# Adding Q rows to gathered P rows inside the gathering DMA, in a graph-attention kernel

## The chip, the cores and the metric

The kernel runs on one core of a Trainium2 chip. The time is the device time of one execution, in microseconds (us). Engines are named as the profile names them: PE (TensorE), DVE (VectorE), ACT (ScalarE), POOL (GpSimd), SP (SyncE); beside them 16 DMA engines move data.

## The reference

There are 512 nodes with 1024 features, and 8704 edges sorted by destination. With h = relu(layernorm(x)), each edge has a logit from its two end nodes, by a weight matrix that depends on the edge's position: the first 256 edges are "hh", the next 1280 "oo", the remaining 7168 "ho".

```python
feat = concat([h[src], h[dst]], axis=1)
e_f  = relu(feat[part] @ W_part + b_part)        # W_part: 2048 x 1024, for hh, oo, ho
logit = (e_f @ W_a + b_a)[:, 0]
alpha = softmax of logit over the edges with the same dst
z = segment_sum(alpha[:, None] * h[src], dst)
out = x + concat([relu([h, z][:128] @ W_hn + b_hn), relu([h, z][128:] @ W_on + b_on)])
```

## The kernel before

**The split of the edge product.** For ho and oo the product of an edge is a sum of two node products: P = h @ W[top half] + b, looked up by src, and Q = h @ W[bottom half], looked up by dst. Both tables, 512 rows of 1024 float32 (4 KB), are made once per kind (`p_ho`, `q_ho`, `p_oo`, `q_oo` in device memory). An edge's logit is then the sum over the features of relu(P[src] + Q[dst]) * w_a. The 256 hh edges are multiplied directly.

**Edge tiles.** A tile is 128 edges, one on each partition. ho has 56 tiles (`T_HO`), oo 10 (`T_OO`), together `T_NODE` = 66; each partition holds a run of consecutive edges (partition p, columns 0 to 55), so that in a run the destination often repeats. `column(n)` (L51) gives the column of tile n: with four slots, each slot walks along a run of its own. For each tile POOL issues three indirect DMAs on its one queue: `p_rows` (L843 to L847) gathers 128 P rows into `gath[:, 0, slot]`; `q_rows` (L849 to L854) gathers Q rows into `gath[:, 1, slot]`; `scatter` (L856 to L859) writes the 128 logits into a 512 x 512 table of pairs. `q_rows` takes its indices from `q_index` (L445 to L450), in which an edge whose destination is that of the slot's last edge has an index out of bounds: that row isn't moved, and the Q row that lies in the slot is used again.

**DVE's part** is `edges(n)` (L464 to L473): it waits for both rows, adds them (L470), and L472 does relu, the product with w_a and the sum in one instruction.

**POOL's order** is written out (L861 to L897): P of tiles 0 to 3 once the P table is stored, Q of tiles 0 to 3 once Q is stored (L866), then for each n from 4: wait for the logits of tile n-4, issue P(n), Q(n), wait until all earlier scatters have landed (`s_scat`), scatter(n-4). In between stand the two hh scatters (`HH_AT`) and the loads of the pair tables.

**DVE's order** is written out too. In the counting stage (L521 to L524) 16 tiles stand between the one-hots (L502) that PE needs to count pairs (L714). Then the weight chunks come: a chunk (1 MB, `raw`, loaded by SP at L204) is split by ACT into a high part (`split_hi`, L240) and by DVE into a low part (`split_lo`, L424), and PE multiplies with both (L664 to L666, three matmuls for each product). `TILES_OO`, `TILES_HH`, `TILES_TOP` and `TILES_G` say how many tiles DVE does before each chunk's `split_lo`: three for each of the 8 chunks of the oo stage, 10 in the hh stage (8 chunks, half the matmuls), 10 in the 8 chunks of the node update's top half, and 2 before each of the first three chunks of the stage after it. So a late gather delays DVE's next `split_lo`, and that delays PE.

**The end.** When all logits are scattered, the tables are loaded, maxima, exponentials and counts give the attention matrix, and PE multiplies it (L810 to L812).

Of the kernel before, what the change touches and what calls it, by code (L numbers as in the profile page):

```python
# [16 lines left out]
P = 128  # L17
N, D = 512, 1024
# [6 lines left out]
T_HH, T_OO, T_HO = E_HH // P, E_OO // P, E_HO // P  # L25
T_ALL = T_HO + T_OO + T_HH
T_NODE = T_HO + T_OO
# [12 lines left out]
ORDER = (1, 2, 3, 0)  # L40
SLOTS = 4
RUN = T_HO // SLOTS
OO_RUNS = (0, 3, 6, 8)
HH_AT = 58
UNCHANGED = 1024.0
EMPTY = -3.0e38
TINY = 1.0e-30
EPS = 1e-5


def column(n):  # L51

    if n < T_HO:
        return RUN * (n % SLOTS) + n // SLOTS
    n -= T_HO
    return T_HO + OO_RUNS[n % SLOTS] + n // SLOTS


def build(nc, x, src, dst, w_chunks, biases, w_a, b_a, out):
    f32, f32r, bf16, f16 = mybir.dt.float32, mybir.dt.float32r, mybir.dt.bfloat16, mybir.dt.float16  # L60
    i32, i16 = mybir.dt.int32, mybir.dt.int16
    ALU = mybir.AluOpType
# [11 lines left out]
    with ExitStack() as ctx:  # L74
        def sb(name, shape, dt):
            return ctx.enter_context(nc.sbuf_tensor(name, shape, dt))
# [9 lines left out]
        def sem(name):  # L86
            return ctx.enter_context(nc.semaphore(name))
# [5 lines left out]
        w_lo = sb("w_lo", [P, SPLIT, KC, HALF], f32r)  # L93
        gath = sb("gath", [P, 2, SLOTS, D], f32)
        feat_hi, partial = shared(("feat_hi", [P, 2 * KT, E_HH], f32r), ("partial", [P, NB, D], f32))
# [25 lines left out]

        q_index = sb("q_index", [P, T_NODE], i32)
        cell = sb("cell", [P, T_NODE], i32)
        logit = sb("logit", [P, T_NODE], f32)
        same = sb("same", [P, T_NODE], f32)
        pair_hh = sb("pair_hh", [P, T_HH], i32)
# [7 lines left out]

        edge_p, edge_q = gath[:, 0], gath[:, 1]
        x_sb = gath[:, 0]
# [19 lines left out]
        s_qrow = [sem(f"q_rows_landed{i}") for i in range(SLOTS)]  # L156
        s_esum, s_logit, s_scat = sem("edge_summed"), sem("logit_ready"), sem("logits_scattered")
        s_node = sem("node_row_ready")
# [229 lines left out]
        def _(dve):  # L388
            steps = [0]

            def step(i):

                steps[0] += 1
                i.then_inc(s_dve, 1)
                dve.wait_ge(s_dve, steps[0])
# [48 lines left out]

            step(nc.vector.tensor_tensor(same[:, 1:T_NODE], f_dst[:, 1:T_NODE], f_dst[:, 0:T_NODE - 1], ALU.is_equal))  # L445
            for first in (*range(0, T_HO, RUN), *(T_HO + at for at in OO_RUNS)):
                i = nc.vector.memset(same[:, first:first + 1], 0.0)
            step(i)
            nc.vector.scalar_tensor_tensor(out=q_index[:, :], in0=same[:, :], scalar=UNCHANGED, in1=f_dst[:, 0:T_NODE],
                                           op0=ALU.mult, op1=ALU.add)  # L450
            nc.vector.scalar_tensor_tensor(out=cell[:, :], in0=f_dst[:, 0:T_NODE], scalar=float(N),
# [12 lines left out]
            def edges(n):  # L464

                slot, at = n % SLOTS, column(n)
                dve.wait_ge(s_prow[slot], 16 * (n // SLOTS) + 16)
                dve.wait_ge(s_qrow[slot], 16 * (n // SLOTS) + 16)
                p, q = edge_p[:, slot], edge_q[:, slot]
                nc.vector.tensor_tensor(p, p, q, ALU.add).then_inc(s_esum, 1)  # L470
                dve.wait_ge(s_esum, n + 1)
                nc.vector.scalar_tensor_tensor(out=p, in0=p, scalar=0.0, in1=wa[:, :], op0=ALU.max, op1=ALU.mult,  # L472
                                               accum_out=logit[:, at:at + 1]).then_inc(s_logit, 1)  # L473

# [341 lines left out]
        def _(pool):  # L816
# [26 lines left out]
            def p_rows(n):  # L843
                kind, slot, at = "ho" if n < T_HO else "oo", n % SLOTS, column(n)
                nc.gpsimd.indirect_dma_start(edge_p[:, slot], None, node_tab[kind][0][:, :],  # L845
                                             bass.IndirectOffsetOnAxis(ap=i_src[:, at:at + 1], axis=0)
                                             ).then_inc(s_prow[slot], 16)  # L847

            def q_rows(n):  # L849

                kind, slot, at = "ho" if n < T_HO else "oo", n % SLOTS, column(n)
                nc.gpsimd.indirect_dma_start(edge_q[:, slot], None, node_tab[kind][1][:, :],  # L852
                                             bass.IndirectOffsetOnAxis(ap=q_index[:, at:at + 1], axis=0),
                                             bounds_check=N - 1, oob_is_err=False).then_inc(s_qrow[slot], 16)  # L854

            def scatter(n):  # L856
                kind, at = "ho" if n < T_HO else "oo", column(n)
                nc.gpsimd.indirect_dma_start(pair_tab[kind][:, :], bass.IndirectOffsetOnAxis(ap=cell[:, at:at + 1], axis=0),  # L858
                                             logit[:, at:at + 1], None).then_inc(s_scat, 16)  # L859

# [5 lines left out]
            pool.wait_ge(s_qst, 32)  # L866
            for n in range(SLOTS):
                q_rows(n)
            for n in range(SLOTS, T_NODE + SLOTS):
# [13 lines left out]
                if n < T_NODE:  # L883
                    p_rows(n)
                    q_rows(n)
                if n > SLOTS:
# [44 lines left out]
```

## Time and profile before

| | us |
|---|---|
| median of 3 runs (567.0 to 568.1) | 567.56 |
| the profiled execution | 567.12 |
| its span, first to last instruction | 565.3 |
| PE busy | 481.7 |
| DVE busy | 360.5 |
| POOL busy | 271.3 |
| ACT busy | 173.3 |
| data moved | 111.27 MB |

The profiled execution agrees with the runs. A matmul's end is modelled in this profile, so PE's busy time is not time at its peak rate. A POOL `DMA_INDIRECT` is the time in which POOL makes the descriptors; the transfer itself runs afterwards in the DMA engines, and "to landing" is the time from issue until its semaphore rises.

### The profile page before, as it was taken

The numbers are of one execution on the slowest core, as the hardware profiler recorded it, in microseconds if no ns is written. First come the engines' busy times: TensorE is split into PE (matmuls) and PEld (weight loads), VectorE is DVE, ScalarE is ACT, GpSimd is POOL, SyncE is SP. The second block draws the span as 40 slices with busy tenths as digits, with TensorE's granted clock in tenths as the row PEclk, the third lists the DMA queues.
The fourth block names the chain that finished last, engine by engine and source line by source line (L and its number), as shares of the span: only waits on it lengthen the run. The fifth ranks groups of instructions, "written<-read, shape, count | busy, mean of one in ns | idle before, by whom it ended". The sixth has DMA issues, their size and how long they took to land.

```text
span 565.3 us, 5665 instructions
## 1 busy us (share of the span) xinstructions
PE 481.7 (85%) x2008; PEld 361.7 (64%) x2008; DVE 360.5 (64%) x516; ACT 173.3 (31%) x236; POOL 271.3 (48%) x221
## 2 busy tenths in 40 slices
PE   2799999989989899897785579786867999999397
PEld 2688888833434488676664467574745888888285
DVE  5713133249987687656675688797874567657644
ACT  3611321457764611221014023222212121443400
POOL 2020000326887867667766777776766563303000
PEclk9999999989998899989988689898989999999689
DMA  8998254762444455766587578678767943200412
GB/s 332 384 425 312 88 177 166 275 222 79 119 117 120 122 182 170 258 235 193 186 266 251 185 241 259 223 251 267 253 233 278 362 154 113 74 1 0 150 56 93
DMA packets 38196, 111.27 MB, mean 197 GB/s; under 512 B 13542, under 2 KB 13542, under 8 KB 32672
## 3 DMA queue, kind: packets, MB, share of 16 engines
q0 software_dynamic: 22576, 45.93, 26.1%
q1 hardware_dynamic: 9888, 53.03, 25.2%
q10 hardware_dynamic: 5712, 12.06, 5.9%
q8 instruction: 11, 0.18, 0.1%
q14 instruction: 9, 0.07, 0.0%
HBM read 123.80 MB, written 15.76 MB: 247 GB/s over the span
## 4 chain that ended last, share of the span: by engine, by line
PE 38%; POOL 25%; issue 15%; DMA 11%; DVE 9%; ACT 1%; POOLq 0%; ACTq 0%; DVEq 0%
PE bank L664 11%; PE bank L666 11%; PE bank L665 11%; POOL pairs_ho L858 9%; POOL gath L845 8%; POOL gath L852 8%; DMA gath<-q_ho,q_index 6%; DMA pairs_ho<-logit,cell 2%; DVE gath L470 2%; DVE gath L472 2%; DVE w_lo L424 2%; PE bank L714 2%; DMA gath<-q_oo,q_index 1%; PE bank L810 1%; PE bank L811 1%
## 5 line engine op out<-in xcount | busy, mean ns | idle before, releaser
L664 PE MATMUL bank<-w_hi,h_t 128*128 128x512 f32 x448 | 180.2, 402 | 30.9 <-DVE w_lo L424 28.6
L665 PE MATMUL bank<-w_lo,h_t 128*128 128x512 f32 x448 | 179.2, 400 | 0.0
L666 PE MATMUL bank<-w_hi,h_t 128*128 128x512 f32 x448 | 178.5, 398 | 0.0
L240 ACT ACTIVATE w_hi<-raw 128x1024 fp32r<-128x1024 f32 x80 | 80.5, 1054 | 276.2 <-PE bank L666 245.8
L424 DVE TENSOR_TENSOR w_lo<-raw,w_hi 128x1024 fp32r<-128x1024 f32 x80 | 95.1, 1228 | 67.5 <-ACT w_hi L240 67.5
L470 DVE TENSOR_TENSOR gath<-gath 128x1024 f32<-128x1024 f32 x66 | 80.9, 1226 | 83.4 <-DMA gath<-q_ho,q_index 58.7
L664 PEld LDWEIGHTS bank<-w_hi,h_t 128*128 128x128 f32 x448 | 86.8, 194 | 54.1 <-DVE w_lo L424 29.2
L845 POOL DMA_INDIRECT gath<-p_ho,i_src x56 | 68.3, 1220 | 89.8 <-DMA p_ho<-stage 65.5
L858 POOL DMA_INDIRECT pairs_ho<-logit,cell x56 | 76.8, 1371 | 48.3 <-DMA pairs_ho<-logit,cell 37.3
L666 PEld LDWEIGHTS bank<-w_hi,h_t 128*128 128x128 f32 x448 | 86.9, 194 | 18.5
L665 PEld LDWEIGHTS bank<-w_lo,h_t 128*128 128x128 f32 x448 | 86.5, 193 | 18.0
L472 DVE SCALAR_TENSOR_TENSOR gath<-gath,wa 128x1024 f32<-128x1024 f32 x66 | 81.1, 1230 | 2.3
L852 POOL DMA_INDIRECT gath<-q_ho,q_index x56 | 69.2, 1236 | 27.9 <-issue 16.8
L714 PE MATMUL bank<-count_buf 128*128 128x512 bf16 x272 | 66.0, 401 | 3.1 <-DVE count_buf L502 2.6
L714 PEld LDWEIGHTS bank<-count_buf 128*128 128x128 bf16 x272 | 26.5, 102 | 41.7 <-DVE count_buf L502 8.9
L292 ACT ACTIVATE count_buf<-node_row,step_at 128x512 bf16<-128x512 f16 x68 | 45.2, 714 | 25.0 <-PE bank L714 25.0
L664 PE MATMUL bank<-w_hi,feat_hi 128*128 128x512 f32 x64 | 28.8, 450 | 20.3 <-DVE w_lo L424 20.3
L664 PEld LDWEIGHTS bank<-w_hi,feat_hi 128*128 128x128 f32 x64 | 13.7, 214 | 25.1 <-DVE w_lo L424 17.8
L665 PE MATMUL bank<-w_lo,feat_hi 128*128 128x512 f32 x64 | 28.1, 438 | 0.0
L666 PE MATMUL bank<-w_hi,feat_lo 128*128 128x512 f32 x64 | 27.5, 430 | 0.0
L502 DVE TENSOR_SCALAR count_buf<-node_row,f_dst 128x512 bf16<-128x512 f16 x68 | 21.6, 364 | 8.4 <-PE bank L714 8.0
L858 POOL DMA_INDIRECT pairs_oo<-logit,cell x10 | 13.5, 1350 | 20.3 <-DMA pairs_oo<-logit,cell 19.4
(118 smaller groups left out, 314.0 us busy)
## 6 DMA issues: line engine op xcount, KB each, us to landing
raw<-w_chunks SPq DMA_DIRECT2D x40, 1024.0 KB, 6.9
gath<-x SPq DMA_DIRECT2D x4, 512.0 KB, 5.1
h_dram<-h_sb SPq DMA_DIRECT2D x1, 2048.0 KB, 14.0
p_ho<-stage ACTq DMA_DIRECT2D x2, 1024.0 KB, 5.5
q_ho<-stage ACTq DMA_DIRECT2D x2, 1024.0 KB, 4.2
p_oo<-stage ACTq DMA_DIRECT2D x2, 1024.0 KB, 8.7
q_oo<-stage ACTq DMA_DIRECT2D x2, 1024.0 KB, 5.4
x_again<-x ACTq DMA_DIRECT2D x2, 1024.0 KB, 6.6
```

Source lines behind the costliest of these rows:

```text
L240: nc.scalar.activation(w_hi[:, c % SPLIT, k], raw[:, c % RAW, k], ACT.Copy).then_inc(s_whi, 1)
L292: i = nc.scalar.activation(rows[:, slot, j, 0], node_row[:, :], ACT.Sign, bias=step_at[:, bass.ds(2 * g + j, 1)])
L424: nc.vector.tensor_tensor(w_lo[:, c % SPLIT, k], raw[:, c % RAW, k], w_hi[:, c % SPLIT, k].bitcast(f32), ALU.subtract).then_inc(s_wlo, 1)
L470: nc.vector.tensor_tensor(p, p, q, ALU.add).then_inc(s_esum, 1)
L472: nc.vector.scalar_tensor_tensor(out=p, in0=p, scalar=0.0, in1=wa[:, :], op0=ALU.max, op1=ALU.mult, accum_out=logit[:, at:at + 1]).then_in ...
L664: nc.tensor.matmul(to, hi, w_hi[:, slot, k], start=first, stop=False)
L665: nc.tensor.matmul(to, hi, w_lo[:, slot, k], start=False, stop=False)
L666: return nc.tensor.matmul(to, lo, w_hi[:, slot, k], start=False, stop=last)
L714: i = nc.tensor.matmul(bank[banks + b][:, :], rows[:, slot, j, 1, b * P:(b + 1) * P], rows[:, slot, j, 0], start=False, stop=False)
L845: nc.gpsimd.indirect_dma_start(edge_p[:, slot], None, node_tab[kind][0][:, :], bass.IndirectOffsetOnAxis(ap=i_src[:, at:at + 1], axis=0)). ...
L852: nc.gpsimd.indirect_dma_start(edge_q[:, slot], None, node_tab[kind][1][:, :], bass.IndirectOffsetOnAxis(ap=q_index[:, at:at + 1], axis=0) ...
L858: nc.gpsimd.indirect_dma_start(pair_tab[kind][:, :], bass.IndirectOffsetOnAxis(ap=cell[:, at:at + 1], axis=0), logit[:, at:at + 1], None). ...
```

## The change

The Q rows have no buffer of their own. `gath` is used as eight slots of one tile each. POOL gathers P(n) into a slot, later waits until it has landed, and issues an indirect DMA with `compute_op=ALU.add`, which adds the Q rows, by dst, to what lies in the slot. DVE's add and the indices that skip repeated Q rows are gone: every Q row of every tile is fetched. The add of tile n-2 (`BEHIND`) is issued after P(n); P runs eight tiles ahead of DVE instead of four. The columns are taken in plain order.

```diff
--- before.py
+++ after.py
@@ -38,22 +38,12 @@
 TILES_G = [2, 2, 2, 0, 0, 0, 0]
 PEAK_HH, PEAK_HO = 3, 4
 ORDER = (1, 2, 3, 0)
-SLOTS = 4
-RUN = T_HO // SLOTS
-OO_RUNS = (0, 3, 6, 8)
+SLOTS = 8
+BEHIND = 2
 HH_AT = 58
-UNCHANGED = 1024.0
 EMPTY = -3.0e38
 TINY = 1.0e-30
 EPS = 1e-5
-
-
-def column(n):
-
-    if n < T_HO:
-        return RUN * (n % SLOTS) + n // SLOTS
-    n -= T_HO
-    return T_HO + OO_RUNS[n % SLOTS] + n // SLOTS
 
 
 def build(nc, x, src, dst, w_chunks, biases, w_a, b_a, out):
@@ -91,7 +81,7 @@
 
         x_again, w_hi = shared(("x_again", [P, NHALF, NB, HALF], f32), ("w_hi", [P, SPLIT, KC, HALF], f32r))
         w_lo = sb("w_lo", [P, SPLIT, KC, HALF], f32r)
-        gath = sb("gath", [P, 2, SLOTS, D], f32)
+        gath = sb("gath", [P, 2, SLOTS // 2, D], f32)
         feat_hi, partial = shared(("feat_hi", [P, 2 * KT, E_HH], f32r), ("partial", [P, NB, D], f32))
         feat_lo, g_on_left, hh_rows, h_sb = shared(("feat_lo", [P, 2 * KT, E_HH], f32r),
                                                    ("g_on_left", [P, 2, NB, HALF], f32r),
@@ -119,10 +109,8 @@
         step_at = sb("step_at", [P, T_ALL], f32)
         f_dst = sb("f_dst", [P, T_ALL], f32)
 
-        q_index = sb("q_index", [P, T_NODE], i32)
         cell = sb("cell", [P, T_NODE], i32)
         logit = sb("logit", [P, T_NODE], f32)
-        same = sb("same", [P, T_NODE], f32)
         pair_hh = sb("pair_hh", [P, T_HH], i32)
         logit_half = sb("logit_half", [P, NHALF, T_HH], f32)
         logit_hh = sb("logit_hh", [P, T_HH], f32)
@@ -132,7 +120,7 @@
         peak = sb("peak", [P, 8, NB], f32)
         den = sb("den", [P, 2, NB], f32)
 
-        edge_p, edge_q = gath[:, 0], gath[:, 1]
+        edge = gath[:, :, :, :].rearrange("p a s d -> p (a s) d")
         x_sb = gath[:, 0]
 
         tab_sb = [stage[:, 0], gath[:, 0, 0:2, :].rearrange("p a (b n) -> p (a b) n", n=N), stage[:, 1]]
@@ -154,7 +142,7 @@
         s_one, s_oused, s_cnt, s_cev = sem("onehot_ready"), sem("onehot_used"), sem("counted"), sem("counts_evacuated")
         s_prow = [sem(f"p_rows_landed{i}") for i in range(SLOTS)]
         s_qrow = [sem(f"q_rows_landed{i}") for i in range(SLOTS)]
-        s_esum, s_logit, s_scat = sem("edge_summed"), sem("logit_ready"), sem("logits_scattered")
+        s_logit, s_scat = sem("logit_ready"), sem("logits_scattered")
         s_node = sem("node_row_ready")
         s_hhlog, s_hhscat = sem("hh_logits_ready"), sem("hh_scattered")
         s_hhev, s_hhhalf = sem("hh_evacuated"), sem("hh_half_logits")
@@ -442,12 +430,6 @@
             step(nc.vector.tensor_copy(f_dst[:, :], i_dst[:, :]))
             nc.vector.tensor_scalar(step_at[:, :], f_src[:, :], -1.0, 0.5, ALU.mult, ALU.add)
 
-            step(nc.vector.tensor_tensor(same[:, 1:T_NODE], f_dst[:, 1:T_NODE], f_dst[:, 0:T_NODE - 1], ALU.is_equal))
-            for first in (*range(0, T_HO, RUN), *(T_HO + at for at in OO_RUNS)):
-                i = nc.vector.memset(same[:, first:first + 1], 0.0)
-            step(i)
-            nc.vector.scalar_tensor_tensor(out=q_index[:, :], in0=same[:, :], scalar=UNCHANGED, in1=f_dst[:, 0:T_NODE],
-                                           op0=ALU.mult, op1=ALU.add)
             nc.vector.scalar_tensor_tensor(out=cell[:, :], in0=f_dst[:, 0:T_NODE], scalar=float(N),
                                            in1=f_src[:, 0:T_NODE], op0=ALU.mult, op1=ALU.add)
             nc.vector.scalar_tensor_tensor(out=pair_hh[:, :], in0=f_dst[:, T_NODE:T_ALL], scalar=float(N),
@@ -463,14 +445,11 @@
 
             def edges(n):
 
-                slot, at = n % SLOTS, column(n)
-                dve.wait_ge(s_prow[slot], 16 * (n // SLOTS) + 16)
+                slot = n % SLOTS
                 dve.wait_ge(s_qrow[slot], 16 * (n // SLOTS) + 16)
-                p, q = edge_p[:, slot], edge_q[:, slot]
-                nc.vector.tensor_tensor(p, p, q, ALU.add).then_inc(s_esum, 1)
-                dve.wait_ge(s_esum, n + 1)
-                nc.vector.scalar_tensor_tensor(out=p, in0=p, scalar=0.0, in1=wa[:, :], op0=ALU.max, op1=ALU.mult,
-                                               accum_out=logit[:, at:at + 1]).then_inc(s_logit, 1)
+                nc.vector.scalar_tensor_tensor(out=edge[:, slot], in0=edge[:, slot], scalar=0.0, in1=wa[:, :],
+                                               op0=ALU.max, op1=ALU.mult, accum_out=logit[:, n:n + 1]
+                                               ).then_inc(s_logit, 1)
 
             split_lo(2)
             split_lo(3)
@@ -841,22 +820,23 @@
                                ).then_inc(s_tab[kind], 16)
 
             def p_rows(n):
-                kind, slot, at = "ho" if n < T_HO else "oo", n % SLOTS, column(n)
-                nc.gpsimd.indirect_dma_start(edge_p[:, slot], None, node_tab[kind][0][:, :],
-                                             bass.IndirectOffsetOnAxis(ap=i_src[:, at:at + 1], axis=0)
+                kind, slot = "ho" if n < T_HO else "oo", n % SLOTS
+                nc.gpsimd.indirect_dma_start(edge[:, slot], None, node_tab[kind][0][:, :],
+                                             bass.IndirectOffsetOnAxis(ap=i_src[:, n:n + 1], axis=0)
                                              ).then_inc(s_prow[slot], 16)
 
-            def q_rows(n):
-
-                kind, slot, at = "ho" if n < T_HO else "oo", n % SLOTS, column(n)
-                nc.gpsimd.indirect_dma_start(edge_q[:, slot], None, node_tab[kind][1][:, :],
-                                             bass.IndirectOffsetOnAxis(ap=q_index[:, at:at + 1], axis=0),
-                                             bounds_check=N - 1, oob_is_err=False).then_inc(s_qrow[slot], 16)
+            def add_q_rows(n):
+
+                kind, slot = "ho" if n < T_HO else "oo", n % SLOTS
+                pool.wait_ge(s_prow[slot], 16 * (n // SLOTS) + 16)
+                nc.gpsimd.indirect_dma_start(edge[:, slot], None, node_tab[kind][1][:, :],
+                                             bass.IndirectOffsetOnAxis(ap=i_dst[:, n:n + 1], axis=0),
+                                             compute_op=ALU.add).then_inc(s_qrow[slot], 16)
 
             def scatter(n):
-                kind, at = "ho" if n < T_HO else "oo", column(n)
-                nc.gpsimd.indirect_dma_start(pair_tab[kind][:, :], bass.IndirectOffsetOnAxis(ap=cell[:, at:at + 1], axis=0),
-                                             logit[:, at:at + 1], None).then_inc(s_scat, 16)
+                kind = "ho" if n < T_HO else "oo"
+                nc.gpsimd.indirect_dma_start(pair_tab[kind][:, :], bass.IndirectOffsetOnAxis(ap=cell[:, n:n + 1], axis=0),
+                                             logit[:, n:n + 1], None).then_inc(s_scat, 16)
 
             pool.wait_ge(s_tabs, 48)
             pool.wait_ge(s_norm, 2)
@@ -864,8 +844,8 @@
             for n in range(SLOTS):
                 p_rows(n)
             pool.wait_ge(s_qst, 32)
-            for n in range(SLOTS):
-                q_rows(n)
+            for n in range(SLOTS - BEHIND):
+                add_q_rows(n)
             for n in range(SLOTS, T_NODE + SLOTS):
                 if n == T_HO:
                     pool.wait_ge(s_pst, 64)
@@ -882,7 +862,8 @@
                 pool.wait_ge(s_logit, n - SLOTS + 1)
                 if n < T_NODE:
                     p_rows(n)
-                    q_rows(n)
+                if n - BEHIND < T_NODE:
+                    add_q_rows(n - BEHIND)
                 if n > SLOTS:
                     pool.wait_ge(s_scat, 16 * (n - SLOTS))
                 scatter(n - SLOTS)
```

## Rows read from the trace of the kernel before

**Rows 1.** The page: busy time of each engine; the costliest groups, busy and mean | idle before.

```profile
PE 481.7 (85%) x2008; PEld 361.7 (64%) x2008; DVE 360.5 (64%) x516; ACT 173.3 (31%) x236; POOL 271.3 (48%) x221
...
L470 DVE TENSOR_TENSOR gath<-gath 128x1024 f32<-128x1024 f32 x66 | 80.9, 1226 | 83.4 <-DMA gath<-q_ho,q_index 58.7
```

**Rows 2.** Waits, 199 to 434 us: who waited for whom, total us, times, longest.

```profile
DVE gath L470 <- DMA gath<-q_ho,q_index: 53.8, 20, 5.6
...
PE bank L664 <- DVE w_lo L424: 45.2, 13, 8.4
POOL pairs_ho L858 <- DMA pairs_ho<-logit,cell: 37.3, 20, 3.1
...
DVE gath L470 <- DMA gath<-q_oo,q_index: 10.9, 2, 7.4
```

**Rows 3.** Timeline of PE: start us, us, engine, line, operation.

```profile
197.20 0.39 PE L666 MATMUL bank<-w_hi,h_t 128*128 128x512 f32 x1
...
204.68 0.39 PE L666 MATMUL bank<-w_hi,h_t 128*128 128x512 f32 x1
```

**Rows 4.** Groups of PE's instructions by line, 199 to 434 us; L665, L666 have like counts.

```profile
L664 PE MATMUL bank<-w_hi,h_t 128*128 128x512 f32 x185 | 75.7, 409 | 24.9 <-DVE w_lo L424 24.8
...
L664 PE MATMUL bank<-w_hi,feat_hi 128*128 128x512 f32 x64 | 28.8, 450 | 20.3 <-DVE w_lo L424 20.3
```

**Rows 5.** Stretches: length, busy of each engine; last columns clock, DMA share, GB/s.

```profile
0.00:50.00 50.00, 36.57 (x150) 30.60 (x151) 24.59 (x61) 18.73 (x26) 7.13 (x14) 1.00 0.91 369
199.00:316.00 117.00, 94.00 (x387) 75.35 (x385) 80.57 (x96) 22.18 (x26) 81.65 (x68) 0.94 0.65 214
...
434.00:480.00 46.00, 44.43 (x189) 36.70 (x190) 32.24 (x40) 7.97 (x10) 26.43 (x21) 0.96 0.59 210
```

**Rows 6.** POOL's three issues: duration min/median/max ns; last row P's landings.

```profile
L845 POOL DMA_INDIRECT gath<-p_ho,i_src x56: 937/966/2016, 101.2 to 397.3; - x56
...
L852 POOL DMA_INDIRECT gath<-q_ho,q_index x56: 986/1005/2062, 117.7 to 398.5; - x56
...
L858 POOL DMA_INDIRECT pairs_ho<-logit,cell x56: 1025/1034/2080, 133.5 to 432.1; - x56
...
DMA to landing us min/median/max: 4.1/5.2/10.3
```

**Rows 7.** Timelines of POOL and DVE near 350 us.

```profile
351.39 1.00 POOL L852 DMA_INDIRECT gath<-q_ho,q_index  x1 [0.31 <-issue]
...
357.41 2.00 POOL L852 DMA_INDIRECT gath<-q_ho,q_index  x1 [0.31 <-issue]
...
356.12 2.41 DVE L424 TENSOR_TENSOR w_lo<-raw,w_hi 128x1024 fp32r<-128x1024 f32 x2
```

**Rows 8.** DMA, 199 to 434 us: totals; queues' packets, MB, share; P gathers issued.

```profile
DMA packets 19192, 54.78 MB, mean 233 GB/s; under 512 B 7766, under 2 KB 7766, under 8 KB 16240
...
q0 software_dynamic: 13472, 25.32, 35.1%
q1 hardware_dynamic: 3312, 24.12, 28.8%
q10 hardware_dynamic: 2400, 5.24, 6.3%
...
gath<-p_ho,i_src POOLq DMA_INDIRECT x37, 5.4
gath<-p_oo,i_src POOLq DMA_INDIRECT x4, 5.1
```

**Rows 9.** Groups of DVE's instructions by line: one that prepares the Q indices.

```profile
L445 DVE TENSOR_TENSOR same<-f_dst 128x65 f32<-128x65 f32 x1 | 0.2, 221 | 0.0
```

**Rows 10.** Counting stage: DVE's groups, 127 to 191 us; PE's count matmuls, all.

```profile
L470 DVE TENSOR_TENSOR gath<-gath 128x1024 f32<-128x1024 f32 x16 | 19.5, 1219 | 4.9 <-DMA gath<-q_ho,q_index 4.9
L502 DVE TENSOR_SCALAR count_buf<-node_row,f_dst 128x512 bf16<-128x512 f16 x58 | 18.4, 362 | 4.1 <-PE bank L714 3.6
...
L714 PE MATMUL bank<-count_buf x272: 376/379/635, 118.3 to 192.3; 128*128 128x512 bf16 x136
```

## The prediction

> **What bounds the kernel now.** I first read the shares of busy time. PE is busy 85% of the span, DVE 64%, POOL 48% [rows 1]. No engine is full over the whole span, so the limit has to be found stage by stage. The DVE add that the change deletes (L470) is 66 instructions of 1226 ns, 80.9 us of DVE time, and DVE stood idle 83.4 us just before them, mostly for Q rows to land [rows 1].
>
> Second, the waits inside the long stretch from 199 to 434 us, where chunks 9 to 33 of the weights meet tiles 16 to 58 of the edges [rows 2]. PE waits 45.2 us for DVE's `split_lo` (L424). DVE waits 53.8 + 10.9 = 64.7 us for gathers. POOL waits 37.3 us for its previous scatter to land. So the chain is POOL and its transfers, then DVE, which runs its tiles and its splits in one written order, then PE.
>
> Third, how much PE has to give. In an unbroken piece the matmul at 197.20 and the one at 204.68 are 33 matmuls apart, 0.227 us each [rows 3]. The stretch records 185 x 3 + 64 x 3 = 747 of them [rows 4], so PE needs 747 x 0.227 = 169 us of the 235. Up to 66 us could be won there, if DVE never came late. From 434 to 480 PE is busy 44.4 of 46 us [rows 5], so the tail is PE's own and I leave it as it is.
>
> Fourth, what POOL does. An issue costs 0.966 us for P (L845), 1.005 for Q (L852), 1.034 for the scatter (L858) [rows 6], with 0.30 us of sequencer time before each. That is 3.9 us a tile at best, against 235 / 43 = 5.5 us taken. Part of the rest is contention: at 351.39, with DVE waiting, L852 takes 1.00 us; at 357.41, under the `TENSOR_TENSOR` of L424, it takes 2.00 [rows 7].
>
> Fifth, the DMA engines. In the stretch they moved 54.78 MB and the three queues show 35.1 + 28.8 + 6.3 = 70% of the 16 engines' time [rows 8], 233 GB/s. They are not the bound yet, but landings are long (P 5.2 us in the median, up to 10.3) [rows 6].
>
> **The change part by part.**
>
> Removed on DVE: L470 and its wait, 1.23 us a tile, 43 tiles in the stretch: 53 us of work. DVE is waiting for rows more than that (64.7 us), so this alone wins nothing while rows come no sooner.
>
> Removed with it: the preparation of `q_index` and `same`, one 0.22 us operation [rows 9] and ten of its size or smaller, under 1 us in all, beside PE's first products. Nothing.
>
> POOL's contention: with L470 gone only L424 can stretch an issue. In 199 to 316 POOL's 68 issues took 81.65 us [rows 5], 1.20 each against 1.0 in the medians, so 0.6 us a tile is lost, and more in the later part. L470 and L424 run about equally often there, so I count half of the loss as gone; what L424 still costs I put at 0.4 us a tile. POOL's floor is then 3.9 + 0.4 = 4.3 us a tile.
>
> Slots: eight tiles deep instead of four. P of tiles 4 to 7 is issued in the gap between 106 and 117.7 us, where POOL waited for the Q store, instead of after it, so 4 x 1.27 = 5 us come off POOL's chain at the start, and later bursts of landing time are ridden out.
>
> Added wait: POOL now waits for P(n-2) to land before it issues the add for n-2. Behind it stand that add, the scatter of n-8 and P(n+1); DVE and the scatter's own successor wait for those. P(n-2) is two rounds, 2 x 5.5 = 11 us, older; the median landing is 5.2, the maximum 10.3. Covered: zero. If P landings double, each excess microsecond is POOL's.
>
> Added bytes, the largest term. Today a Q row is skipped when the edge before it in the partition had the same destination. In the stretch queue 0 moved 25.32 MB; 41 P gathers of 128 x 4 KB are 21.5 and one table is 1.05, so Q moved only 2.8 MB for 42 gathers [rows 8]. Afterwards each is whole, 22.0 MB: 19.2 MB more. And each row is not copied but added: the engine must fetch the Q row and also fetch the P row that stands in the slot. No row shows such a transfer. The low bound is a plain gather, 74.0 MB in all for the stretch; two fetches make it 96.0; a high bound is a gather's time three times, 118 MB. I take two fetches, since two rows have to be read for one written.
>
> Rate of the engines: in the first 50 us 369 GB/s at a share of 0.91 [rows 5], which is 405 at 1.0; in the stretch 233 at 0.70, which is 331 at 1.0 (its packets include waiting in contention). I take the middle, 370. Then 96.0 MB need 259 us, where the stretch takes 235: **+24 us**. The ends: 237 us (+2) at 405, 290 us (+55) at 331. The work of one tile there is 259 / 43 = 6.0 us, above POOL's 4.3 and PE's 169 / 43 = 3.9, so the engines set the pace.
>
> On this point the trace is silent and the Trainium skill is not: "Collectives: The Full Stack" (The bandwidth ceiling, on why ReduceScatter is half of AllGather) says that an add in the DMA engine costs no ALU time but needs two source reads in the same read ring, and so runs at half the rate of a copy. By that page the sum is the +24 above, by a free add it would be the first rival.
>
> The counting stage, 120 to 191 us: DVE alternates one-hots (58 x 0.36 us) and 16 tiles, of which the add is 1.2 us each [rows 10], and PE's 272 count matmuls need only 272 x 0.227 = 62 us of its 74. There are no weight loads; P and the add are 3 x 0.524 = 1.57 MB a tile, 4.2 us at 370, and POOL's 3.9 is near it. Six adds can be issued from 117.7; the last 10 tiles at 4.2 us end at about 125 + 42 + 6 = 173, so PE becomes the bound and the stage ends near 184: **-7 us**. Bounds -10 and 0.
>
> Sum: 24 - 7 = +17. The profiled execution took 567.1 us (span 565.3 and 1.8 around it), 0.4 below the median of 567.56. 567.1 + 17 = **584**.
>
> **Rivals.**
>
> Forecast's case, two fetches, the engines the bound, 0.55. Its own range is 235 to 290 us for the stretch less 7 (or 0): 562 to 622.
>
> An add as cheap as a plain gather, 0.30. For it: the engines' share is only 0.70 today, and nothing in the trace excludes that the second fetch, which is from on-chip memory, runs beside the first. Then 74.0 MB at 370 are 200 us, POOL's 43 x 4.3 + 5 for the two scatters of HH are 190, PE's 169 is below: the stretch falls by 35, and with the 7 the time is 525 (549 at 331 GB/s, 515 if POOL alone counts). The case decides below about 1.6 fetches per add: (235 x 0.370 - 52) / 22 = 1.6, where 52 MB is everything but the adds.
>
> An add dearer than two fetches, 0.15. Its place is either the engines (three fetches: 118 / 0.370 = 319 us, +84, near 650) or POOL's issue, if it has to write more than one descriptor per row on the reading side: an add of 3.0 us instead of 1.0 makes 43 x 6.3 = 271 us, +36, near 600. I price it at 630. Against it: nothing in the trace; for it: only that there is no row.
>
> The order of the adds against P (two tiles behind) as a bound of its own would need P to land later than 11 us; that is a consequence of saturated engines and is inside the first and third case.
>
> **How the numbers follow.** A measurement of this kernel can tell 0.2%, 1.1 us, from no change. The forecast case gives slower 0.47, no difference 0.03, faster 0.05 (its low end plus the counting stage); the cheap add is faster, 0.30; the dear one slower, 0.15. Together 0.35, 0.03, 0.62. Both signs have weight. The range takes most of the cheap case and part of the dear one, 518 to 636; the likeliest case's own is 562 to 622.
>
> **What the changed profile would show.** DMA share near 0.95 in 199 to 434, queue 0 with about 75 MB by the bytes it writes and a time share above 45%; DVE at L472 still waiting over 60 us, for adds; L852's successor at about 1.0 us an issue, landing in 7 us or more; scatters landing in 5 us or more; tile 15 done near 173 to 180 us. If instead DMA share stays near 0.8, PE's waits for L424 shrink from 45 us below 20 and tile 58 is done before 400 us, the cheap case holds and 584 is wrong by the doubled fetch. If POOL's adds last 2 us or more each, the dear one holds.

## The result and the profile after

The changed kernel takes 626.88 us (621.55 to 632.55, 4 runs) against 567.83 (567.0 to 568.69): the ratio is 1.103, interval 1.093 to 1.114, 59 us slower. The forecast was 584, slower; the sign came true, and the loss was three and a half times the forecast one. One of the four runs, 632.55, was in a slower state of the chip; without it the median is 624.86 and the loss 57 us.

The page of the changed kernel, to be read against [rows 1]: its span, busy shares, the slices of DMA share, the queues, and the chain that ended last.

```profile
span 627.1 us, 5463 instructions
...
PE 494.9 (79%) x2008; PEld 370.2 (59%) x2008; DVE 280.7 (45%) x440; ACT 173.3 (28%) x236; POOL 296.5 (47%) x221
...
DMA  9995328899988899988899899899969997401302
...
q0 software_dynamic: 22576, 74.50, 49.6%
...
DMA 45%; PE 28%; POOL 15%; issue 7%; DVE 4%; ACT 1%; ACTq 0%; DVEq 0%; POOLq 0%
DMA pairs_ho<-logit,cell 42%; PE bank L643 7%; PE bank L645 7%; PE bank L644 7%; POOL gath L832 5%; POOL pairs_ho L838 4%; POOL gath L824 4%; PE bank L693 2%; DMA gath<-q_oo,i_dst 2%; PE bank L789 1%; PE bank L790 1%; PE bank L791 1%; DMA pairs_hh<-logit_hh,pair_hh 1%; DVE stats L388 1%; POOL pairs_oo L838 1%
```

DVE's 80 us are gone and DMA share is at 0.8 to 0.9 from the first gather on. The surprise is the last line: 42% of the span's chain is one kind of transfer, the scatter of 128 four-byte logits. It moves next to nothing.

Groups of POOL's and DVE's instructions (columns as in [rows 1]), and who waited for whom over the whole span, as in [rows 2].

```profile
L450 DVE SCALAR_TENSOR_TENSOR gath<-gath,wa 128x1024 f32<-128x1024 f32 x66 | 80.8, 1224 | 223.3 <-DMA gath<-q_ho,i_dst 174.1
L832 POOL DMA_INDIRECT gath<-q_ho,i_dst x56 | 90.5, 1615 | 26.2 <-issue 16.8
...
DVE gath L450 <- DMA gath<-q_ho,i_dst: 174.1, 46, 8.8
PE bank L643 <- DVE w_lo L412: 95.4, 18, 11.4
POOL pairs_ho L838 <- DMA pairs_ho<-logit,cell: 91.2, 40, 5.8
```

DVE, relieved of an add, now waits 223 us before its tiles where it waited 83 [rows 1]. POOL waits 91 us for ho scatters and, on a line not shown, 23 for oo ones: 114 against 57 (37 and 19) before.

The stretch from 199 to 434 us, with the columns of [rows 5], and the tiles that DVE finished in it (this answer's groups by line):

```profile
199.00:434.00 235.00, 160.79 (x606) 127.10 (x605) 93.72 (x129) 40.21 (x44) 150.10 (x107) 0.83 0.94 254
...
L450 DVE SCALAR_TENSOR_TENSOR gath<-gath,wa 128x1024 f32<-128x1024 f32 x36 | 44.1, 1225 | 141.2 <-DMA gath<-q_ho,i_dst 141.2
```

36 tiles in 235 us are 6.5 us each, where 43 were done before, 5.5 each. When DVE's tiles start, first and last, tells that the whole loss lies there: before (L472) and in the changed kernel (L450).

```profile
L472 DVE SCALAR_TENSOR_TENSOR gath<-gath,wa x66: 1224/1225/1274, 128.9 to 477.8; 128x1024 f32<-128x1024 f32 x66
L450 DVE SCALAR_TENSOR_TENSOR gath<-gath,wa x66: 1206/1226/1268, 126.8 to 541.0; 128x1024 f32<-128x1024 f32 x66
```

The last tile starts 63 us later, and what comes behind it takes 86 us in place of 88. The granted TensorE clock is hardly the cause: its mean in the stretch fell from 0.93 to 0.83 of full speed, but PE stood idle 74 of the 235 us there (47 before), for `split_lo`, and DVE waits for ACT's high parts 67.5 us in all, as before. The stretch in the kernel before:

```profile
199.00:434.00 235.00, 187.51 (x747) 148.96 (x745) 168.48 (x198) 52.28 (x56) 164.06 (x128) 0.93 0.70 233
```

The chain of waits between 230 and 262 us shows the mechanism, start and length of each piece:

```profile
230.93 6.55 DMA pairs_ho<-logit,cell
237.48 0.27 issue
237.75 8.35 DMA pairs_ho<-logit,cell
246.10 0.27 issue
246.37 6.39 DMA pairs_ho<-logit,cell
```

Each piece runs from a scatter's issue to its landing, and the next scatter starts at once. POOL's own timeline of the same moment:

```profile
237.75 1.00 POOL L838 DMA_INDIRECT pairs_ho<-logit,cell  x1 [2.23 <-DMA pairs_ho<-logit,cell]
239.06 0.96 POOL L824 DMA_INDIRECT gath<-p_ho,i_src  x1 [0.30 <-issue]
240.33 1.56 POOL L832 DMA_INDIRECT gath<-q_ho,i_dst  x1 [0.30 <-issue]
246.37 1.64 POOL L838 DMA_INDIRECT pairs_ho<-logit,cell  x1 [4.48 <-DMA pairs_ho<-logit,cell]
```

The scatter issued at 237.75 stands on the same queue as the rows and adds issued before it. POOL issues one P, one add, and has then to wait 4.48 us until it has landed. (These are among the longer ones; the median of all 66 is below.) One round trip of a scatter per tile is a floor for the tile rate, whatever DVE does.

### The profile page after: what moved, and what is told of

Read it like the earlier page. It is cut to its first block, busy times and chain, and to the rows that moved or that the text cites. A ratio compares the mean times of both kernels' runs of the same rounds, so it can differ in the third digit from the quotient of the medians.

```text
span 627.1 us, 5463 instructions
## 1 busy us (share of the span) xinstructions
PE 494.9 (79%) x2008; PEld 370.2 (59%) x2008; DVE 280.7 (45%) x440; ACT 173.3 (28%) x236; POOL 296.5 (47%) x221
## 3 DMA queue, kind: packets, MB, share of 16 engines
q0 software_dynamic: 22576, 74.50, 49.6%
## 4 chain that ended last, share of the span: by engine, by line
DMA 45%; PE 28%; POOL 15%; issue 7%; DVE 4%; ACT 1%; ACTq 0%; DVEq 0%; POOLq 0%
DMA pairs_ho<-logit,cell 42%; PE bank L643 7%; PE bank L645 7%; PE bank L644 7%; POOL gath L832 5%; POOL pairs_ho L838 4%; POOL gath L824 4%; PE bank L693 2%; DMA gath<-q_oo,i_dst 2%; PE bank L789 1%; PE bank L790 1%; PE bank L791 1%; DMA pairs_hh<-logit_hh,pair_hh 1%; DVE stats L388 1%; POOL pairs_oo L838 1%
## 5 line engine op out<-in xcount | busy, mean ns | idle before, releaser
L643 PE MATMUL bank<-w_hi,h_t 128*128 128x512 f32 x448 | 186.5, 416 | 61.8 <-DVE w_lo L412 59.6
L644 PE MATMUL bank<-w_lo,h_t 128*128 128x512 f32 x448 | 183.5, 410 | 0.0
L645 PE MATMUL bank<-w_hi,h_t 128*128 128x512 f32 x448 | 182.8, 408 | 0.0
L450 DVE SCALAR_TENSOR_TENSOR gath<-gath,wa 128x1024 f32<-128x1024 f32 x66 | 80.8, 1224 | 223.3 <-DMA gath<-q_ho,i_dst 174.1
L643 PEld LDWEIGHTS bank<-w_hi,h_t 128*128 128x128 f32 x448 | 89.9, 201 | 87.1 <-DVE w_lo L412 60.1
L838 POOL DMA_INDIRECT pairs_ho<-logit,cell x56 | 81.7, 1458 | 96.1 <-DMA pairs_ho<-logit,cell 91.2
L412 DVE TENSOR_TENSOR w_lo<-raw,w_hi 128x1024 fp32r<-128x1024 f32 x80 | 94.3, 1220 | 67.5 <-ACT w_hi L228 67.5
L832 POOL DMA_INDIRECT gath<-q_ho,i_dst x56 | 90.5, 1615 | 26.2 <-issue 16.8
L645 PEld LDWEIGHTS bank<-w_hi,h_t 128*128 128x128 f32 x448 | 89.7, 200 | 20.1
L644 PEld LDWEIGHTS bank<-w_lo,h_t 128*128 128x128 f32 x448 | 90.1, 201 | 19.1
L824 POOL DMA_INDIRECT gath<-p_ho,i_src x56 | 62.6, 1118 | 80.4 <-DMA p_ho<-stage 63.6
L693 PE MATMUL bank<-count_buf 128*128 128x512 bf16 x272 | 64.4, 397 | 4.9 <-DVE count_buf L481 4.9
L838 POOL DMA_INDIRECT pairs_oo<-logit,cell x10 | 12.2, 1223 | 26.8 <-DMA pairs_oo<-logit,cell 23.3
L832 POOL DMA_INDIRECT gath<-q_oo,i_dst x10 | 18.3, 1834 | 3.0 <-issue 3.0
```

Source lines behind the costliest of these rows:

```text
L412: nc.vector.tensor_tensor(w_lo[:, c % SPLIT, k], raw[:, c % RAW, k], w_hi[:, c % SPLIT, k].bitcast(f32), ALU.subtract).then_inc(s_wlo, 1)
L450: nc.vector.scalar_tensor_tensor(out=edge[:, slot], in0=edge[:, slot], scalar=0.0, in1=wa[:, :], op0=ALU.max, op1=ALU.mult, accum_out=logi ...
L643: nc.tensor.matmul(to, hi, w_hi[:, slot, k], start=first, stop=False)
L644: nc.tensor.matmul(to, hi, w_lo[:, slot, k], start=False, stop=False)
L645: return nc.tensor.matmul(to, lo, w_hi[:, slot, k], start=False, stop=last)
L693: i = nc.tensor.matmul(bank[banks + b][:, :], rows[:, slot, j, 1, b * P:(b + 1) * P], rows[:, slot, j, 0], start=False, stop=False)
```

## The experiments

Two theories stood at the start: A, the engines' time for the second fetch; B, the round trip of the scatter. A third, C, was POOL's dearer issue (1.57 us in the median for the add, 1.005 for Q before [rows 6]).

**Plain Q gathers in the changed kernel** (the sum is left out):

```diff
                 nc.gpsimd.indirect_dma_start(edge[:, slot], None, node_tab[kind][1][:, :],
                                              bass.IndirectOffsetOnAxis(ap=i_dst[:, n:n + 1], axis=0),
-                                             compute_op=ALU.add).then_inc(s_qrow[slot], 16)
+                                             ).then_inc(s_qrow[slot], 16)
```

> The kernel after, with the add taken out of the Q transfer: it gathers every Q row plainly over the P row in the same slot, with the same waits (the sum P + Q is left out). Theory A (the engines' time for the second fetch is the bound): queue 0's work per tile falls from two kinds of packets, 159 and 328 ns, to two of 159 ns, 3.9 to 2.5 us of all 16 engines, and most of the 59 us comes back: 560 to 580 us. Theory B (POOL waits for each scatter to land, whatever is in the queue, and the round trip of that wait is the bound): the landing of a scatter shortens only by what stands ahead of it, some 1.4 us a tile of 6 to 7, and the time stays near 600 us. Theory C (POOL's dearer issue, 1.57 against 1.0 us, is the bound): the issue falls back to 1.0 and the time falls by 66 x 0.57 = 38 us or less, to about 590.

Measured 569.32 us, ratio 1.003 (0.999 to 1.007): with the same bytes written, the same rows fetched and the same waits, 58 us come back, which is all that the change had lost and no more. Queue 0 of its page:

```profile
q0 software_dynamic: 22576, 74.50, 37.7%
```

The same line of the kernel before:

```profile
q0 software_dynamic: 22576, 45.93, 26.1%
```

From the shares, an added row can be priced. Before, queue 0 moved 45.93 MB in 26.1% of 16 x 565.3 us; here 74.50 MB in 37.7% of 16 x 570.9. The difference is 1083 engine-us for 28.57 MB, 6975 rows of 4 KB: 155 ns a plain row. In the changed kernel the same queue has 49.6% of 16 x 627.1, 1533 engine-us more for the 66 x 128 adds: 181 ns each on top. An add is 155 + 181 = 336 ns, 2.2 plain rows; these are estimates, since a packet's time includes waiting. The packet records say the same: with plain gathers most rows of queue 0 take 159 ns each, and with the add a second group of them takes 328, 2.1 times. So the forecast's doubled fetch was right, and yet the cheap add gave 569 and not the forecast 525. Something other than the engines held it there.

**All Q rows in the kernel before:**

```diff
-            nc.vector.scalar_tensor_tensor(out=q_index[:, :], in0=same[:, :], scalar=UNCHANGED, in1=f_dst[:, 0:T_NODE],
+            nc.vector.scalar_tensor_tensor(out=q_index[:, :], in0=same[:, :], scalar=0.0, in1=f_dst[:, 0:T_NODE],
```

> The kernel before, with every Q row fetched (no index out of bounds), four slots, DVE's add kept. It shows what the 28 MB of Q rows cost by themselves. Theory A: the engines have room at 70% share for plain rows, so 567 to 580 us. Theory B: each scatter lands later by a Q gather's 1.3 us and POOL waits for it, up to 66 x 1.3 = 85 us less what is hidden: 590 to 620.

592.22 us, ratio 1.047 (1.035 to 1.058). The 28.6 MB by themselves cost 24 us, although the DMA share in 199 to 434 was only 0.82. B's range began at 590 and A's ended at 580. What B says of the scatters can be read in four kernels that all have one chain of them. The landing is the time from a scatter's issue to the last rise of its semaphore, the median over the tiles:

| kernel | landing, us | POOL's waits for scatters, us | time, us |
|---|---|---|---|
| before | 3.2 | 57 | 568 |
| before, all Q rows | 4.3 | 77 | 592 |
| changed, plain Q gathers | 4.1 | 74 | 569 |
| changed | 5.6 | 114 | 627 |

The more work the queue has, the later the same 512 bytes land. The time follows with one exception: the changed kernel with plain gathers has no add on DVE and twice the slots.

**Two chains of scatters in the changed kernel** (odd tiles' logits go to a table that is not loaded):

```diff
-                nc.gpsimd.indirect_dma_start(pair_tab[kind][:, :], ...
-                                             logit[:, n:n + 1], None).then_inc(s_scat, 16)
+                nc.gpsimd.indirect_dma_start((pair_tab, odd_tab)[n % 2][kind][:, :], ...
+                                             logit[:, n:n + 1], None).then_inc(s_scat[n % 2], 16)
...
-                if n > SLOTS:
-                    pool.wait_ge(s_scat, 16 * (n - SLOTS))
+                if n > SLOTS + 1:
+                    pool.wait_ge(s_scat[(n - SLOTS) % 2], 16 * ((n - SLOTS) // 2))
```

> The kernel after, with odd tiles' logits scattered into a second pair table with a semaphore of its own, so that a scatter waits for the one two tiles earlier and no longer for the last one (half of the logits are left out of the result). Theory A: the engines are full, so POOL's wait moves elsewhere and the time stays within 10 us of 627. Theory B: POOL's 114 us of waits for scatters go and the time falls to 580 to 600.

577.12 us, ratio 1.016 (1.006 to 1.027): 50 us less than the changed kernel, in a kernel that does the same transfers. A is refuted as the only bound, and B's range, 580 to 600, was a little too high. POOL's waits for scatters fall from 114 to 27 us, while a scatter's median landing rises from 5.6 to 8.2: it is the broken wait that helps, not a faster scatter into a second table. What is left is A's, as the stretch, the slices and queue 0 of its page say:

```profile
199.00:434.00 235.00, 179.52 (x677) 141.04 (x676) 109.69 (x148) 47.25 (x52) 175.19 (x122) 0.86 1.01 293
...
DMA  8997334979999999999999999999979994200412
...
q0 software_dynamic: 22576, 74.50, 50.8%
```

Now the engines are full: a share of 1.01 (packets' times can overlap, so it can pass 1), 40 tiles in 235 us, 5.9 each. The forecast had reckoned 6.0 for exactly this state. The step from 0.94 and 6.5 us a tile looks small; a share close to 1 doesn't by itself say that the engines set the pace.

**The same in the kernel before:**

> The same second table and semaphore in the kernel before (half of the logits are left out of the result). There POOL waits 57 us for scatters. Theory B, for this kernel: it falls by 10 to 30 us, since DVE waits 83 us for Q rows that POOL issues late. Theory A has no say here; if it stays at 567, the waits for scatters were covered even before.

538.51 us, ratio 0.954 (0.945 to 0.964): 29 us faster by the medians, 26 by the ratio. In the stretch DVE finishes 48 tiles instead of 43 (in the profiled execution, 530.57 us, the fastest of the four), and PE waits for `split_lo` 19.9 us in all:

```profile
DVE gath L471 <- DMA gath<-q_ho,q_index: 36.1, 20, 4.2
...
PE bank L665 <- DVE w_lo L425: 19.9, 10, 5.4
```

So the wait for scatters, 37 us in [rows 2], was a bound before the change already, and I had read that row and not priced it.

**Plain gathers and two chains together:**

> Plain Q gathers in the kernel after (the sum left out) and odd tiles' logits in a second table with a semaphore of its own. By the forecast's arithmetic for a cheap add, 74 MB at 370 GB/s, this should be 525. B2 says the same from the runs: with neither the double fetch (3.9 to 2.5 us a tile) nor the scatter's round trip, POOL's issue of 3.9 to 4.3 us is the bound as in the run of the kernel before with two chains (538.5), so 525 to 545. If double fetch and round trip were two bounds in series, their gains add: 627 - 58 - 50 = 519.

535.39 us, ratio 0.939 (0.930 to 0.948). Only with both does the rival's 525 come near. The gains, 58 and 50, don't add: their sum would give 519. With two chains the add costs 577 - 535 = 42, with one chain 58. PE is now busy 215 of the 235 us and 48 tiles take 4.9 us each, so POOL's issue of 3.9 to 4.3 us is not the bound that I expected; PE's own work is near.

```profile
199.00:434.00 235.00, 214.65 (x900) 173.03 (x900) 135.23 (x182) 62.33 (x70) 171.40 (x140) 0.96 0.93 348
```

**Four slots in the changed kernel** (`SLOTS = 4`):

> The kernel after with four slots instead of eight (BEHIND stays 2, so an add can be only two tiles ahead of DVE). Theory B2 (after the first four runs: the engines and the scatter's round trip set POOL's pace, some 6.7 us a tile, and DVE waits for rows all the time): depth is worth little in the steady state, 627 to 645. Rival: depth rides out the long landings, and without it the add's 8 us round trip is seen at every second tile: 660 to 720.

636.71 us, ratio 1.125 (1.116 to 1.134). Half the depth costs 10 us. In the long stretch DVE does 36 tiles with either depth; the last count matmul starts at 203.6 us, against 193.3 with eight slots. Eight slots help little where the supply is late on every tile.

**DVE's add left out, all Q rows fetched, in the kernel before:**

```diff
-                nc.vector.tensor_tensor(p, p, q, ALU.add).then_inc(s_esum, 1)
-                dve.wait_ge(s_esum, n + 1)
-                nc.vector.scalar_tensor_tensor(out=p, in0=p, scalar=0.0, in1=wa[:, :], op0=ALU.max, op1=ALU.mult,
+                nc.vector.scalar_tensor_tensor(out=p, in0=q, scalar=0.0, in1=wa[:, :], op0=ALU.max, op1=ALU.mult,
```

> The kernel before with all Q rows fetched (592) and DVE's add left out (L472 reads Q alone, P is not used). It shows what taking 66 x 1.23 us from DVE is worth by itself. If the sum of DVE's work counted, up to 43 us in the long stretch: 550. B2: DVE waits for POOL anyway; only the stretched issues (0.4 us a tile, 25 us in all) and the 1.2 us between landing and the freed slot come back: 570 to 585.

578.02 us, ratio 1.021 (1.013 to 1.029): 14 us less than 592, for 80.9 us of DVE work. POOL's groups of the two kernels, first with the add, then without it:

```profile
L852 POOL DMA_INDIRECT gath<-q_ho,q_index x56 | 74.3, 1327 | 27.9 <-issue 16.9 <-DMA q_ho<-stage 11.0
...
L858 POOL DMA_INDIRECT pairs_ho<-logit,cell x56 | 83.4, 1490 | 62.8 <-DMA pairs_ho<-logit,cell 53.8 <-issue 8.9
```

```profile
L856 POOL DMA_INDIRECT pairs_ho<-logit,cell x56 | 82.6, 1474 | 56.6 <-DMA pairs_ho<-logit,cell 49.6 <-issue 7.0
L850 POOL DMA_INDIRECT gath<-q_ho,q_index x56 | 65.5, 1170 | 27.9 <-issue 16.8 <-DMA q_ho<-stage 11.0
```

The Q issue falls from 1.33 to 1.17 us, the scatter's hardly: the stretched issues return 9 us on these lines and not the 25 I had reckoned with. (The profiled execution without the add took 571.7 us, 6 below its median.)

**The add four tiles behind P** (`BEHIND = 4`):

> The kernel after with the add issued four tiles behind P instead of two (BEHIND = 4). If POOL's wait for P rows to land were part of the loss, P is now some 27 us old and the time falls by 5 to 20 us. If it was covered, as the forecast had it, 620 to 635: nothing, or a little worse since an add is issued later for its tile.

627.69 us, ratio 1.111 (1.103 to 1.119), the changed kernel's own time. The wait for P rows was covered, as forecast; nor does the changed kernel's list of waits show POOL waiting for P rows.

**A longer POOL issue with plain gathers:**

```diff
+                if n:
+                    pool.wait_ge(s_pad, n)
+                nc.gpsimd.memset(pad[:, :], 0.0).then_inc(s_pad, 1)
```

> The run with plain Q gathers (569), and behind each Q issue a POOL memset of a scratch tile, about 0.4 us and its start, so that POOL's time for a tile is about as long as with the add's dearer issue (1.57 against 1.0 us). If the dearer issue was part of the 58 us between plain gather and add, the time rises toward 590 to 600. If the engines' second fetch alone made it, 569 to 576.

576.87 us, ratio 1.018 (1.010 to 1.025), against 1.003 without the memset: 0.015 x 565 = 8 us. The memset took 444 ns in the mean:

```profile
L839 POOL MEMSET pad<- 128x384 f32 x66 | 29.3, 444 | 0.0
```

66 x 0.44 = 29 us more of POOL's time cost 8. The result lies just above the bound set for A alone and far under C's. I estimate from it that of the 58 us between plain gather and add something near 8 to 11 belongs to the issue (1.57 against 0.94 us is 0.63, somewhat more than the memset), the rest to the engines and to the scatter's longer way behind them.

**A version that beats both.** The kernel before, its scatters in two chains, and both tables used: two more tables are cleared, two more loaded into slots that are free after the last tile, and DVE takes the maximum of the two.

```diff
+                    dve.wait_ge(s_odd[0], 16)
+                    step(nc.vector.tensor_tensor(tab_sb[0], tab_sb[0], odd_sb[0], ALU.max))
...
+            dve.wait_ge(s_odd[1], 16)
+            step(nc.vector.tensor_tensor(tab_sb[1], tab_sb[1], odd_sb[1], ALU.max))
...
+                if n == T_NODE + SLOTS - 1:
+                    load_odd(0)
```

> The kernel before with two pair tables for ho and for oo, even and odd tiles, each with its own chain of scatters; both are cleared at the start and loaded at the end, and DVE takes their maximum before it goes on. Nothing is left out. The two chains gave 538.5; four more 1 MB transfers (2.6 us each at 405 GB/s, beside other work) and two DVE maxima of 2.4 us near the end: 538 to 550. If the merges fall on the end of the chain in full, 550 to 555.

542.13 us (537.28 to 545.0, 6 runs), ratio 0.954 (0.948 to 0.960): 26 us faster than the kernel before, 85 faster than the changed one. The merged tables cost 4 us against the run that leaves half of the logits out, which is within its spread; one of the two maxima in DVE's timeline:

```profile
470.53 2.36 DVE L428 TENSOR_TENSOR w_lo<-raw,w_hi 128x1024 fp32r<-128x1024 f32 x2 [3.31 <-ACT w_hi L244]
472.81 2.29 DVE L615 TENSOR_TENSOR stage<-stage,gath 128x2048 f32<-128x2048 f32 x1
475.13 2.29 DVE L601 TENSOR_REDUCE peak<-stage 128x4 f32<-128x2048 f32 x1
```

Taken in order, the runs split the change: all Q rows +24 (568 to 592), DVE's add out -14 (578), eight slots, the Q gather behind its P row and the plain column order together -9 (569), the add in the engines instead of a copy +58 (627). The first three come from runs beside different sets of the kernel before (568.1, 568.7), so each is good to some 5 us.

## Why the prediction was right and wrong

**What bounds the kernel before.** "POOL and its transfers, then DVE, then PE" is right. Incomplete was the reading of POOL: the row "POOL waits 37.3 us for its previous scatter" was named as a link and given no price. The run with two chains prices it at 29 us.

**DVE's add, worth nothing alone.** Nearly: 14 us with its contention, out of 80.9, measured where all Q rows are fetched.

**POOL's contention.** Half of the loss was to go with L470; on the Q and scatter lines of the run without the add only 9 us did. What stays was put at 0.4 us a tile and is about 0.7: P, add and scatter take 1.12, 1.62 and 1.46 us in the mean, 4.2 together, against 0.96, 1.56 and 1.00 undisturbed, 3.5. The ground was false too: "only L424 can stretch an issue", but the reduction that stays on DVE (now L450) does it as well (below). None of this entered the sum.

**The slots.** 10 us in the changed kernel; the forecast counted 5 at the start and an unpriced help later.

**The added wait.** Zero, as forecast.

**The doubled fetch.** Right: 2.2 plain rows by the shares, 2.1 by the packets. Here the Trainium skill's rule ("Collectives: The Full Stack", The bandwidth ceiling) agrees: it says that the add needs two source reads in one read ring and runs at half the rate. That the two reads share a ring is not shown by any run here.

**The sum of the stretch, +24.** This is the step that failed. It divides bytes by a rate and so takes the engines to be fed at every moment ("so the engines set the pace"). With two chains they are: 5.9 us a tile measured, 6.0 reckoned, 577 in place of 584. In the changed kernel they are not: a scatter waits behind the rows and adds on its queue, POOL can have only one in flight, and a longer queue makes the round trip longer. It costs 50 us in the changed kernel and 29 before. The added transfers therefore came in twice, as work of the engines and as delay of a serial wait: the add costs 42 us with two chains, where the wait is broken, and 58 with one. I had foreseen "scatters landing in 5 us or more" and given no term for it; they land in 5.6 in the median.

**The counting stage, -7.** Wrong, and by the same cause: with two chains it came out. With P and the add at 4.2 us a tile PE should have become the bound. The groups of DVE there, as in [rows 10]:

```profile
L450 DVE SCALAR_TENSOR_TENSOR gath<-gath,wa 128x1024 f32<-128x1024 f32 x16 | 19.5, 1222 | 19.4 <-DMA gath<-q_ho,i_dst 19.4
L481 DVE TENSOR_SCALAR count_buf<-node_row,f_dst 128x512 bf16<-128x512 f16 x58 | 18.9, 371 | 11.7 <-PE bank L693 9.4 <-issue 2.3
```

The 19.5 us of adds saved there turned into 19.4 us of waiting for adds. PE's last count matmul started at 193.3 us, at 192.3 before [rows 10]. With two chains of scatters in the changed kernel it started at 185.7, near the forecast end at 184:

```profile
L694 PE MATMUL bank<-count_buf x269: 376/379/634, 117.9 to 185.7; 128*128 128x512 bf16 x135
```

**The rivals.** The cheap add was priced at 525 from 200 us of the engines and 190 of POOL's issues, without the round trip, and the run gave 569. The dear one (630, 0.15) has the right time and the wrong cause: neither a third fetch nor an issue of 3 us exists, the issue takes 1.57. That 627 lies inside 518 to 636 is luck: only this rival carries the range so far, and the likeliest case's own ended at 622. The sign rested on the doubled fetch, and that held. The 1.1 us by which "no difference" was set apart can't be told either: runs of the kernel before, beside the experiments, go from 561 to 578 us.

**The signs.** Most of the forecast's own came true, though its sum was wrong: a DMA share of 0.94 in the stretch (0.95 forecast), queue 0 at 49.6% with 74.5 MB, DVE waiting far over 60 us. Against it stood the issue of the add (1.57 us for 1.0), its landing (6.2 us in the median for 7 or more), and tile 15, which DVE started at 192.3 us and which should have been done by 180.

What stays open: how the 58 us of the add divide exactly between engines and issue, since the memset is shorter than the difference and no run lengthened one issue alone.

## What to carry to other kernels

When a tiny transfer shares a queue with large ones and the issuer must see it land before it goes on, price its round trip, not its bytes: what is put ahead of it can be paid again as delay. Breaking such a chain in two (here a second table and semaphore) was worth 29 us where moving 80 us of vector work into the transfers cost 59. An add inside a gather should be reckoned as two gathers. It could pay where DVE, not the supply of rows, is what others wait for; that is argued, no run here has such a kernel.

## What was not expected of the hardware

An added 4 KB row takes 336 ns of an engine against 155 for a gathered one, and the issue of an add 1.57 us against 0.94 for a plain gather with the same indices (median of the run with plain gathers):

```profile
L832 POOL DMA_INDIRECT gath<-q_ho,i_dst x56: 935/941/2002, 120.3 to 403.1; - x56
```

A scatter's issue rose from a median of 1.03 us [rows 6] to 1.53, though it is the same instruction; with plain gathers in the changed kernel it is 1.43, so the add is not what makes it. DVE's timeline around the two scatters shown above, which took 1.00 us at 237.75 and 1.64 at 246.37:

```profile
235.87 1.23 DVE L450 SCALAR_TENSOR_TENSOR gath<-gath,wa 128x1024 f32<-128x1024 f32 x1 [0.85 <-DMA gath<-q_ho,i_dst]
...
245.90 1.23 DVE L450 SCALAR_TENSOR_TENSOR gath<-gath,wa 128x1024 f32<-128x1024 f32 x1 [8.79 <-DMA gath<-q_ho,i_dst]
```

The first began 0.65 us after DVE's instruction had ended, the second while it had 0.76 us to go, and that one is 0.64 us longer. It is the same contention that [rows 7] show under `TENSOR_TENSOR`. The scatters of the changed kernel bear it out: the 8 whose first microsecond had under 0.1 us of a `TENSOR_TENSOR` or `SCALAR_TENSOR_TENSOR` of DVE beside it took at most 1.03 us, the 52 with over 0.4 us of one took 1.64 in the median, though a few of these still took 1.0. Scatter and L450 now tend to start together, because the same landing front on queue 0 releases both; that last step is argued from the two lists of waits and was not tried by itself. The Trainium skill ("SBUF — State Buffer", Who interferes with whom) has a rule that fits both rows: a DVE instruction with two inputs in on-chip memory contends with a GpSimd instruction that reads there. Further on the section infers that making descriptors does not suffer from `tensor_tensor`; here it does, 2.00 us against 1.00 [rows 7], and the measurement decides.
